# Queries and keys stored rows first: seven loads a group in place of ten, with the repeated key parts read by a zero stride

## The reference, cut to what matters

```python
h = layernorm(x) * (1 + ca) + sa                       # x: 4 batches x 1024 rows x 128
Q, K, V = heads(h, Wq, bq), heads(h, Wk, bk), heads(h, Wv, bv)     # 16 heads of 8
scores  = einsum('bhid,bhjd->bhij', Q, K) / sqrt(8)
QJ      = einsum('bhid,hde->bhie', tanh(Q), J_attn)
scores += lambda_attn * einsum('bhie,bhje->bhij', QJ, tanh(K))
probs   = softmax(where(causal, -inf, scores))
x = x + ga * (probs @ V @ Wo.T + bo)
h = layernorm(x) * (1 + cb) + sb
# each row goes to one of 8 experts (argmax of h @ centroids.T): layernorm, 128 -> 512 -> 128, gated sum
x = x + gb * ffn(h)
```

## Time and profile before

| | before |
|---|---|
| median of 3 runs (lowest to highest) | 845.47 us (844.82 to 854.59) |
| the profiled execution | 847.08 us, span 845.2 us |
| TensorE busy | 694.1 us (82%), mean granted clock 0.917 |
| VectorE busy | 620.3 us (73%) |
| ScalarE busy | 455.9 us (54%) |
| GpSimd busy | 250.6 us (30%) |
| SyncE's transfers (q1) | 41904 packets, 67.56 MB, 34.2% of 16 engines |
| loads of keys | 96 of 128 KB, 7.3 us from issue to landing |
| loads of queries | 16 of 384 KB, 5.1 us; 16 of 256 KB, 5.7 us; 16 of 128 KB, 6.0 us |

### The profile page before, as it was taken

How to read it: one execution, slowest core, us unless ns; L and a number is a source line. 1 busy time by engine, 2 the same in 40 slices (tenths; PEclk the granted TensorE clock), 3 DMA queues, 4 the chain that set the end, 5 groups by cost and what they waited for, 6 DMA issues and landing times.

```text
span 845.2 us, 17049 instructions
## 1 busy us (share of the span) xinstructions
PE 694.1 (82%) x5087; PEld 348.3 (41%) x5087; DVE 620.3 (73%) x1485; ACT 455.9 (54%) x1077; POOL 250.6 (30%) x210
## 2 busy tenths in 40 slices
PE   3517597999999899888798987999988879886694
PEld 1314143333343334233333333433423326876694
DVE  6698977778778887878487878778887812786453
ACT  0213065667665575546456754557564668644482
POOL 5205803930000860114028502030001400453643
PEclk9758589999999999989799999999999979997898
DMA  9389190419533237525403392436302243621520
GB/s 260 132 209 255 43 177 1 124 55 168 113 69 61 77 104 145 97 53 134 102 14 92 90 183 57 86 109 144 123 16 90 113 147 105 194 65 66 191 77 12
DMA packets 51305, 91.96 MB, mean 109 GB/s; under 512 B 9005, under 2 KB 24945, under 8 KB 50700
## 3 DMA queue, kind: packets, MB, share of 16 engines
q1 hardware_dynamic: 41904, 67.56, 34.2%
q0 software_dynamic: 6400, 17.86, 6.8%
q10 hardware_dynamic: 2908, 5.41, 2.0%
HBM read 51.05 MB, written 37.90 MB: 105 GB/s over the span
## 4 chain that ended last, share of the span: by engine, by line
PE 51%; DVE 22%; issue 11%; DMA 6%; SPq 5%; ACT 2%; DVEq 1%; POOL 0%; ACTq 0%; POOLq 0%
PE PS L989 13%; PE PS L1014 12%; PE PS L952 10%; DVE PS L1443 5%; PE PS L1065 4%; PE PS L1076 3%; DVE arenaB L1111 3%; SPq L376 3%; DVE block_max L1450 2%; PE PS L1018 2%; DMA arenaA<-mrow 2%; ACT arenaA L785 2%; PE PS L892 2%; DMA arenaB<-r_den 1%; DVE arenaA L1111 1%
## 5 line engine op out<-in xcount | busy, mean ns | idle before, releaser
L785 ACT ACTIVATE arenaA<-PS 128x512 f32<-128x512 f32 (+3 forms) x768 | 332.0, 494 | 251.4 <-PE PS L1018 190.4
L1443 DVE CUSTOM_DVE_ANT_0 PS<-PS,mask 128x1024 f32<-128x1024 f32 (+3 forms) x256 | 261.3, 1037 | 71.9 <-PE PS L952 63.9
L1014 PE MATMUL PS<-arenaA 99*128 99x512 bf16 (+3 forms) x768 | 225.4, 340 | 17.3 <-DMA arenaA<-mrow 7.9
L952 PE MATMUL PS<-arenaA 96*128 96x512 bf16 (+3 forms) x768 | 202.7, 341 | 36.3 <-DVE maxima L1443 19.8
L989 PE MATMUL PS<-arenaA,Vs 128*9 128x512 f32 (+3 forms) x1536 | 164.2, 504 | 0.0
L1014 PEld LDWEIGHTS PS<-arenaA 99*128 99x128 bf16 x768 | 73.8, 99 | 207.3 <-ACT arenaA L785 122.5
L1450 DVE TENSOR_REDUCE block_max<-PS 128x8 f32<-128x1024 f32 (+1 forms) x96 | 100.3, 1045 | 24.3 <-PE PS L957 23.1
L952 PEld LDWEIGHTS PS<-arenaA 96*128 96x128 bf16 x768 | 66.5, 101 | 107.3 <-DVE maxima L1443 46.5
L1018 PE MATMUL PS<-after,identb 128*128 128x128 bf16 x512 | 107.6, 227 | 0.0
L574 POOL TENSOR_TENSOR arenaB<-arenaB 128x1024 f32<-128x1024 f32 x13 | 27.9, 2144 | 197.6 <-ACT arenaB L724 197.5
L677 POOL DMA_INDIRECT out_dram<-arenaA x46 | 46.1, 1001 | 98.2 <-DVE arenaA L1111 94.8
(11 more groups left out here) (179 smaller groups left out, 726.7 us busy)
## 6 DMA issues: line engine op xcount, KB each, us to landing
arenaA<-k_parts SPq DMA_DIRECT2D x96, 128.0 KB, 7.3
arenaA<-by_expert SPq DMA_DIRECT2D x46, 192.5 KB, 3.4
o_raw<-OT SPq DMA_DIRECT2D x32, 256.0 KB, 2.2
arenaA<-q_parts SPq DMA_DIRECT2D x16, 384.0 KB, 5.1
q_parts<-arenaB POOLq DMA_DIRECT2D x18, 256.0 KB, 3.8
k_parts<-arenaB POOLq DMA_DIRECT2D x18, 256.0 KB, 3.8
arenaA<-q_parts SPq DMA_DIRECT2D x16, 256.0 KB, 5.7
w_turned<-arenaA SPq DMA_DIRECT2D x2, 2048.0 KB, 9.4
```

The costliest lines, as they stand in the source:

```text
L785: a.activation(PT[:, u % EB, h, off:HALF], PS[:, 4 + n % SB_, off:HALF], ACT.Exp).then_inc(exp_ok, 1)
L952: last = mm(PS[:, place + c0 // HALF, at:at + c1 - c0], SQ(g, h)[0:KROWS, t * P:(t + 1) * P], SK(g, h)[0:KROWS, c0:c1], start=(at == 0), s ...
L1014: last = mm(bank[:, off:HALF], SK(g, h)[0:MROWS, kb * P:(kb + 1) * P], SQ(g, h)[0:MROWS, qc * HALF + off:(qc + 1) * HALF], start=True, sto ...
L1443: v.tensor_tensor_reduce(out=src, in0=src, in1=mask[:, S - n:S], scale=1.0, scalar=-3e38, op0=ALU.add, op1=ALU.max, accum_out=maxima[:, pl ...
```

## The change

The two DRAM tensors get the shape `[B, 3, ROW, H, S]`: rows outside, heads inside. The four heads of a group lie together in DRAM for one row, 8 KB. A load of keys takes a part once in DRAM and repeats it 3, 2 or 1 times, by a dimension with stride zero ahead of the rows, so that six key loads become three. The stores write the same values to their new places. The counts that are waited for go from 10 to 7.

```diff
-        q_parts = dram("q_parts", [B, H, 3, ROW, S], BF16)
-        k_parts = dram("k_parts", [B, H, 3, ROW, S], BF16)
+        q_parts = dram("q_parts", [B, 3, ROW, H, S], BF16)
+        k_parts = dram("k_parts", [B, 3, ROW, H, S], BF16)
...
+        LOADS = 7
...
             Q_ROWS = ((0, 0, 3), (3, 0, 2), (5, 0, 1))
-            K_ROWS = ((0, 0, 1), (1, 0, 1), (2, 0, 1), (3, 1, 1), (4, 1, 1), (5, 2, 1))
+            K_ROWS = ((0, 0, 3), (3, 1, 2), (5, 2, 1))
 
             def load_group(b, g):
-                for side, src, terms in ((0, q_parts, Q_ROWS), (1, k_parts, K_ROWS)):
-                    for t, j, n in terms:
-                        sp.dma_start(stacks[t * ROW:(t + n) * ROW, g, side, :, :],
-                                     src[bass.ds(b, 1), g * HG:(g + 1) * HG, j:j + n, :, :].rearrange("a h j r q -> (a j r) h q"))\
-                            .then_inc(stack_in[g], 16)
+                heads = slice(g * HG, (g + 1) * HG)
+                for t, j, n in Q_ROWS:
+                    sp.dma_start(stacks[t * ROW:(t + n) * ROW, g, 0, :, :],
+                                 q_parts[bass.ds(b, 1), j:j + n, :, heads, :].rearrange("a j r h q -> (a j r) h q")).then_inc(stack_in[g], 16)
+                for t, j, n in K_ROWS:
+                    one = k_parts[bass.ds(b, 1), j, :, heads, :]
+                    sp.dma_start(stacks[t * ROW:(t + n) * ROW, g, 1, :, :],
+                                 (one.to_broadcast([n, ROW, HG, S]) if n > 1 else one).rearrange("t r h q -> t r (h q)")).then_inc(stack_in[g], 16)
...
-                    sp.dma_start(dst[0, :, j, off:off + HD, :], T16[:, k, j, :]).then_inc(parts0_out, 16)
+                    sp.dma_start(dst[0, j, off:off + HD, :, :].rearrange("r h q -> h r q"), T16[:, k, j, :]).then_inc(parts0_out, 16)
...
-                        pool.dma_start(dst[bass.ds(b, 1), :, j, off:off + HD, :].rearrange("a h r q -> (a h) r q"),
+                        pool.dma_start(dst[bass.ds(b, 1), j, off:off + HD, :, :].rearrange("a r h q -> (a h) r q"),
...
-                    pe.wait_ge(stack_in[g], (loads + 1) * 10 * 16)
+                    pe.wait_ge(stack_in[g], (loads + 1) * LOADS * 16)
...
-                            dve.wait_ge(stack_in[g], b * 10 * 16)
+                            dve.wait_ge(stack_in[g], b * LOADS * 16)
```

## The result

| | before | the change |
|---|---|---|
| median | 845.14 us (4 runs) | 882.3 us (4 runs, 880.93 to 884.58) |
| ratio | | 1.0463, 95% interval 1.0418 to 1.0507 |
| the profiled execution | 847.08 us, span 845.2 | 884.58 us, span 882.8 |
| SyncE's transfers (q1) | 41904 packets, 67.56 MB, 34.2% | 31488 packets, 67.55 MB, 28.6% |

What follows compares the result with a forecast made beforehand. Bound: TensorE's chain (matmuls half), with thin cover where loads are waited for. Prologue 2.5 + first batch 5.7 + clock 2 = 10.2 us on the profiled 847.08, which is 1.6 above the median: 855.7, predicted 855.5; range 842.5 to 868.

Steps and rivals of the forecast that it cites:

- Layout, stores and issues count nothing: Group loads and part stores: three issues fewer worth under 1 us, counted as nothing; stores of the parts 0.
- Larger pieces "may" be faster: Group loads: 8 KB pieces instead of 2 KB may raise one busy engine from 10.6 to 26.8 GB/s, or not.
- 3 and 2 engines, the same ones: Merged key loads: 48 rows on 3 engines, 32 on 2, the same two carrying 319 KB each; 85 small packets.
- Rival A: No narrowing, or key loads on engines that don't overlap: burst ends before 213, 840.5 to 846 us; chance 0.18.
- The first group of a burst needs 14.5 us: First of two queued group loads: 14.5 us, between 12.8 and 15.6; today one group takes 9.6 us.
- Prologue +2.5: Group 0's load in the prologue lands later and TensorE waits uncovered: between +1.5 and +3.2 us, taken as +2.5.
- First batch +5.7 + 2: First batch, third group: `mrow` transfers land at 221.8, not 216.12, +5.7 us; half clock after TensorE's idle adds 2.
- just in time: First batch's burst: its first load lands at 207.4, before the next batch's group 0 maximum runs at 208.51.
- Later bursts hidden: Bursts at 327.88 and 492.75: need 30.3 us, `mrow` lands 38.3 and 39.0 after first issue; 8 us spare, cost 0.
- Everything but two places is covered: Only prologue and first batch cost time; group 1's load and single loads behind third and fourth groups are covered.
- Rival B: Narrow loads under 26.8 GB/s an engine: total 10.2 + 99x, x us per piece over 0.305; over 2% slower; chance 0.17.
- a first wait of over 10 us: Sign of Rival B: the first wait for a group load, 5.7 us before, at the prologue's end, exceeds 10 us.

Runs made afterwards that it cites:

- seven wide ones: The change with the 16 rows outermost and the zero-stride repeat second, so every load runs on 16 engines, against the kernel before: ratio 0.9998.
- one group at a time: The change with SyncE waiting for group 0's load before issuing group 1's, in prologue and first batch's burst, against the kernel before: ratio 1.0354.

## Why the prediction was wrong, point by point

- **Layout, stores and issues count nothing: right.** Ten loads in the new layout and seven wide ones give 0.9994 and 0.9998.
- **Larger pieces "may" be faster: not so.** I took 10.6 GB/s for one engine as perhaps the price of a 2 KB piece. With 8 KB it stayed (168 to 178 GB/s in all). Other partitions for the same loads did change it (165 to 223 GB/s), so at least part of the limit lies in which partitions the loads fill; that it is the whole limit is not shown.
- **3 and 2 engines, the same ones: right**, and with it the direction. The completions were 85, as written down. The share fell, but after ten us and not five, and to 0.19 and not 2/16: three engines were at work, not two. With one group at a time the share does fall on to 0.07, so the third one is likely to have been busy with pieces of the next group. Rival A had 0.18 and is refuted.
- **The first group of a burst needs 14.5 us: the step that failed.** It took some 22 (23.4 and 23.5 from the first issue to the landing). I let the two engines run at 26.8 GB/s nearly as soon as the queries were through. The traffic of the other engines was priced too low: the rates of the earlier trace rows already showed that all 16 engines together are held at 180 GB/s, and as the others run ahead into the next group's queries this common phase lasts ten microseconds (2 to 3 us of the error). And two of the copies go through the same way into SBUF, which the sum didn't have (about 3 us). With both taken away the landing comes 17.2 us after the first issue, against 16.3 in the prediction's sum.
- **Prologue +2.5:** the wait grew by 10.3, and narrow loads there alone cost 6.5.
- **First batch +5.7 + 2:** the bursts alone cost 15. The sum had the `mrow` transfers (4.9 us more on the last, of which TensorE waited 4.0), but called the maxima of the next batch "just in time" at 1 us of slack, with a load time that was 8 us short; they stood still for 6.5. So TensorE fell to half clock twice and not once, and that cost 5.6 us where the sum had 2.
- **Later bursts hidden: nearly right.** From group 3 of batch 1 to that of batch 2 the delay grew by 1.4 us. The prediction gave them 8 us to spare and the burst used most of it: in batch 1 the share is still 0.12, two engines, at 390 to 392 us, when `mrow` is issued, 34 us after the burst's first issue.
- **Everything but two places is covered: the second step that failed.** I compared the single loads only with the next `mrow`, and the loads of groups 2 and 3 in the prologue are not in the sum at all. Two other waiters were there: VectorE, which may overwrite the values only after those two loads (0.5%), and, in the same queue behind group 3's keys, the load of the denominators (0.8%), which the last body needs sooner than the others. The code shows both; I had followed each queue only as far as TensorE's waits.
- **Rival B** named the right side, over 2% slower, and gave it 0.17. One of its signs, a first wait of over 10 us, came true (16.0). Its threshold, a piece of 0.375 us on average, was passed: 23.5 against 16.3 us for 33 pieces of keys is 0.2 us more a piece. By its own formula, 10.2 + 99 x 0.2, that is 30 us or 875; but I priced it only up to 0.43 us a piece, 868, and ended the range there. The two waiters above (1.3%, 11 us) are in no term of it, so that it comes this near to 882 is in part luck.

## What to carry to other kernels

A zero-stride repeat belongs behind the rows, never in front of them: the same seven loads with the rows outermost cost nothing, with the repeat outermost 4 to 5%. A transfer on a few engines must be priced by the busiest engine, with the traffic that shares its way. Then every waiter behind it in the same queue counts, small transfers for other engines too, in the body in which they are due earliest. And for loads that fill fewer than 128 partitions, the partitions they go to can matter more than the size of the pieces (165 to 223 GB/s against no gain from 8 KB pieces).

## What the runs showed of the hardware that was not expected

- With two or three engines at work, a piece of 8 KB from DRAM takes 0.31 us on an engine, and 0.62 on each of two that write to partitions 0 to 15 and 32 to 47 at the same time.
- A load of 192 rows of 8 KB and the values runs at 154 to 181 GB/s with all engines busy, with ten issues and pieces of 2 KB as with seven and pieces of 8 KB. Moving the 48-row load from partitions 0 to 47 to 32 to 79 (and the 32-row load to 0 to 31) raised this to 223 GB/s in the prologue and brought the landing from 12.9 us after the first issue (53.11 to 66.04) to 10.6 (55.26 to 65.86).
- SyncE itself was held up when two narrow group loads were queued: one issue took 7.33 us and the next 3.57, where the earlier trace rows has a median of 0.4 for a load of keys. This is seen in the change's timeline above and was not tested apart.
